# Loading a quarter of the Toeplitz rows in the first 20 ring blocks, and copying the other quarters on chip

## The chip, the cores and the metric

The kernel runs on one core of a Trainium2 chip. The metric is the device time of one execution in microseconds (us). Besides the unprofiled runs there is one profiled execution, from whose trace all rows below are read. The engines are PE (TensorE), ACT (ScalarE), DVE (VectorE), POOL (GpSimd) and SP (SyncE, which here only issues DMAs).

## The reference

Two layers with a residual each, on x of shape (128 batch, 128 time, 512 channels):

```
# layer 0: causal convolution of length 128 per channel (weights cond[k, d]), projection, state recurrence
conv = conv_b + sum(x_pad[:, k:k+L, :] * cond[k] for k in range(128))
proj = conv @ Wp + bp                    # 512 -> 2*64
B_t, C_t = softplus(proj[..., :64]), tanh(proj[..., 64:])
u = x @ Ws + bs
state = decay * state + dt * B_t * u_t;  y_t = C_t * state      # over time
x = x + (y @ Wo + bo)
# layer 1: tanh recurrence over time, h0 = cond
h = tanh(h @ Wh + x_t @ Wx + b)
x = x + h
```

The change touches only the convolution. For one channel d it is a matrix product over time: out[b, l] = sum over p of x_rev[p, b] * T[p, l], where T[p, l] is element p + l of a row of 256 numbers (127 zeros, the 128 weights of the channel reversed, one zero). T is 128 x 128; entries with p + l < 127 are zero, and a row further down is the row above it moved one column to the left.

## The kernel before

The first part of the kernel convolves, transposes and projects. Channels are taken in four chunks c of 128. A chunk is loaded in 16 ring blocks of CH = 8 channels, so there are 64 blocks n = 0 to 63. The ring in SBUF has RING = 4 slots; block n lies in slot n % 4. Each slot holds two halves: `t_part`, the Toeplitz matrices of the eight channels (128 partitions x 1024 floats, 512 KB), and `x_part`, the reversed inputs of the eight channels (512 KB). The Toeplitz rows are read from a small array `hankel` in HBM by a DMA whose rows overlap (`toeplitz`), so that 512 KB are written for very few distinct bytes. Channels are interleaved in pairs (index i), so a row of a pair is 256 floats, and a block has 4 pairs (index j).

SP issues both loads of a block with `load_ring`: first the Toeplitz rows (L254), then x (L255). The first four blocks are issued at once, with a small load `vec` after block 1 and Wp (`wp_f`, L261) after block 3. Block n from 4 on is issued when PE has finished block n - 4 (`conv_done`). Later in the same queue come the weights of the other layers, after blocks 20, 24 and 28. Before, both loads of a slot count on one semaphore, `ring_loaded`.

PE multiplies in `convolution(c, m)`: four channels d into one PSUM bank `CONV[m % 4]`, each channel one f32 matmul of x (weights) with T (moving), which the trace shows as two instructions at L672. A block is two such banks, 16 instructions. m runs over BANKS = 32 for a chunk. Before bank m PE waits until bank m - 4 was emptied. In chunk 0 nothing else runs on PE: `for m in range(BANKS): convolution(0, m)`. ACT empties the even banks (`copy_conv`, L383) and DVE the odd ones (L501), in order, into `conv`.

After chunk 0 PE waits for Wp and its split into a high and a low half (`wp_ready`, made by POOL at L311 and L313), and then, for c = 0 to 2 and each m, runs `turn(c, m)` (four transposes of the finished chunk, L687), `convolution(c + 1, m)` and `project(c, m - 1)` (three matmuls of 512 columns, L700 to L703). ACT and DVE copy and split the turned banks and add the projections. The order on each engine is written out by hand, with semaphore waits. Chunk 3 is turned and projected last, and a loop over 32 groups of 4 time steps (the recurrences) makes up the rest of the time from about 260 us on.

At the start DVE and ACT also compute a few rates from `vec` (L487 to L496, L376, L378), and POOL makes the identity matrix (L305, L307). The function `kernel` lays the inputs out on the host, among them `x_rev`.

Of the kernel before, what the change touches and what calls it, by code (L numbers as in the profile page):

```python
# [8 lines left out]
ALU = mybir.AluOpType  # L9
ACT = mybir.ActivationFunctionType  # L10

BATCH = 128
TIME = 128
D = 512
N = 64
P = 128
KC = D // P
RING = 4
CH = 8
PER_BANK = 4  # L20
BANKS = P // PER_BANK
# [4 lines left out]
LAST = KC - 1  # L26
# [2 lines left out]
SLOTS = 4  # L29
PAIRS = BANKS // 2  # L30
LAG = 2
LOAD = 2 * 16
DMA = 16


def wait(engine, sem, value):

    if not isinstance(value, int) or value > 0:
        engine.wait_ge(sem, value)


def build(nc, x_rev, x_dtb, hankel, h0_t, vectors, Wp, Ws, Wo, Wx, Wh, b, out):
# [6 lines left out]
    with ctx:  # L49
# [3 lines left out]
        def sem(name):  # L53
            return ctx.enter_context(nc.semaphore(name))
# [90 lines left out]
        def f(ap):  # L145
            return ap.bitcast(F32)

        def t_part(slot):
            return ring[:, slot, 0].rearrange("p (j l i) -> p j l i", j=CH // 2, i=2)

        def x_part(slot):
            return ring[:, slot, 1].rearrange("p (d b) -> p d b", d=CH)

# [22 lines left out]
        def turned_slot(c, m):  # L176
            return turned[:, (BANKS * c + m) % SLOTS]

        ring_loaded = [sem(f"ring_loaded{i}") for i in range(RING)]
        conv_done = sem("conv_done")  # L180
        conv_copied_act = sem("conv_copied_act")
        conv_copied_dve = sem("conv_copied_dve")
# [59 lines left out]
        def toeplitz(n):  # L242

            return bass.AP(hankel.tensor, n * (CH // 2 * 4 * P), [[2, P], [4 * P, CH // 2], [1, 2 * TIME]])

        block = ctx.enter_context(nc.Block())

        @block.sync
        def _(sp):
            def load_ring(n, slot):
                sp.dma_start(ring[:, slot, 0].rearrange("p (j k) -> p j k", j=CH // 2), toeplitz(n)).then_inc(ring_loaded[slot], DMA)  # L254
                sp.dma_start(x_part(slot), x_rev[:, bass.ds(n * CH, CH), :]).then_inc(ring_loaded[slot], DMA)  # L255

            for n in range(RING):
                load_ring(n, n)
                if n == 1:
                    sp.dma_start(vec[:], vectors).then_inc(vec_loaded, DMA)  # L260
            sp.dma_start(wp_f[:], Wp.rearrange("(c p) n -> p c n", p=P)).then_inc(wp_loaded, DMA)  # L261
            for n in range(RING, D // CH):
                sp.wait_ge(conv_done, CH // PER_BANK * (n - RING + 1))
                load_ring(n, n % RING)
                if n == 20:
                    sp.dma_start(wo_f[0:N, :], Wo).then_inc(ws_wo_loaded, DMA)
                    sp.dma_start(ws_f[:], Ws.rearrange("(c p) n -> p c n", p=P)).then_inc(ws_wo_loaded, DMA)
                if n == 24:
                    sp.dma_start(wx_f[:], Wx.rearrange("(c p) n -> p c n", p=P)).then_inc(wx_loaded, DMA)
                if n == 28:  # L270
                    sp.dma_start(wh_f[:], Wh.rearrange("(c p) n -> p c n", p=P)).then_inc(wh_loaded, DMA)
                    sp.dma_start(h0_f[:], h0_t.rearrange("(c p) b -> p c b", p=P)).then_inc(h0_loaded, DMA)

            def load_x(g, slot):
                sp.dma_start(x_f[slot][:], x_dtb[:, bass.ds(g * G, G), :].rearrange("(c p) t b -> p c t b", p=P))\
                  .then_inc(x_loaded[slot], DMA)


            sp.wait_ge(conv_done, BANKS * KC - 4)
            load_x(0, 0)  # L280


            sp.wait_ge(turn_done, BANKS * LAST + 24)
            load_x(1, 1)
            sp.dma_start(b_rows[:], b.partition_broadcast(P)).then_inc(b_loaded, DMA)

            def stores_and_loads(g, par, first, last, q):
                if not (last or (isinstance(g, int) and g == GROUPS - 2)):

                    sp.wait_ge(x1_ready, KC * (g + 1))  # L290
                    load_x(g + 2, par)

                for s in range(0, G, 1 if last else G):
                    n = 1 if last else G
                    sp.wait_ge(out_ready, G * g + s + n)
                    sp.dma_start(out[:, bass.ds(g * G + s, n), :].rearrange("(c p) t b -> p c t b", p=P),
                                 x1_f[par][:, :, s:s + n]).then_inc(stored[par], DMA)

            groups(sp, stores_and_loads)
            sp.wait_ge(stored[0], DMA * (GROUPS // 2))  # L300
            sp.wait_ge(stored[1], DMA * (GROUPS // 2 - 1 + G))

        @block.gpsimd
        def _(pool):
# [2 lines left out]
            nc.gpsimd.affine_select(out=ident[:], in_=ident[:], compare_op=ALU.not_equal, fill=1.0, base=0,  # L307
                                    pattern=[[-1, P]], channel_multiplier=1).then_inc(ident_ready, 1)

            pool.wait_ge(wp_loaded, DMA)  # L310
            nc.gpsimd.tensor_copy(wp_hi[:], wp_f[:, 0:LAST]).then_inc(wp_ready, 1)  # L311
            pool.wait_ge(wp_ready, 1)
            nc.gpsimd.tensor_tensor(wp_lo[:], wp_f[:, 0:LAST], f(wp_hi[:]), ALU.subtract).then_inc(wp_ready, 1)  # L313

            pool.wait_ge(ws_wo_loaded, 2 * DMA)
            nc.gpsimd.tensor_copy(ws_hl[:, :, 0:N], ws_f[:]).then_inc(pool_step, 1)
            pool.wait_ge(pool_step, 1)
# [54 lines left out]
        def _(act):  # L372

            nc.scalar.preload_act_table_set("natural_log_exp_and_others")
            act.wait_ge(rate_step, 1)
            nc.scalar.activation(rates_e[:], rates[:, 0:2], ACT.Exp).then_inc(rate_act, 1)  # L376
            act.wait_ge(rate_act, 1)
# [2 lines left out]
            def copy_conv(c, m):  # L380

                act.wait_ge(conv_done, BANKS * c + m + 1)
                nc.scalar.copy(conv_room(c, m), conv_out(c, m))\  # L383
                  .then_inc(conv_copied_act, 1)

            def copy_turned(c, m):

                act.wait_ge(turn_done, BANKS * c + m + 1)
                out = turned_slot(c, m) if c == LAST else turned_hl[:, 0, m % 2]
                nc.scalar.activation(out, turn_bank(c, m)[:], ACT.Identity, bias=conv_b[:, c:c + 1])\  # L390
                  .then_inc(turn_copied, 1)

            act.wait_ge(vec_loaded, DMA)
            for m in range(0, BANKS, 2):
                copy_conv(0, m)
            for c in range(KC - 1):
                for m in range(BANKS):
                    copy_turned(c, m)
                    copy_conv(c + 1, m)
            nc.scalar.preload_act_table_set("exp_and_others")  # L400

# [81 lines left out]

        @block.vector
        def _(dve):
            dve.wait_ge(vec_loaded, DMA)
            nc.vector.scalar_tensor_tensor(out=rates[:, 0:2], in0=logs, scalar=-1.0, in1=logs, op0=ALU.mult, op1=ALU.min)\  # L487
              .then_inc(rate_step, 1)
# [10 lines left out]
            def copy_conv(c, m):  # L499
                dve.wait_ge(conv_done, BANKS * c + m + 1)  # L500
                nc.vector.tensor_copy(conv_room(c, m), conv_out(c, m))\  # L501
                  .then_inc(conv_copied_dve, 1)
# [15 lines left out]
                  .then_inc(turn_rest, 1)  # L518

            for m in range(1, BANKS, 2):  # L520
                copy_conv(0, m)
            for c in range(KC - 1):
                for m in range(BANKS):
                    turn_rest_of(c, m)
                    if m > 0:
                        add_proj(c, m - 1)
                add_proj(c, BANKS - 1)
                if c == 1:

                    dve.wait_ge(ws_wo_loaded, 2 * DMA)  # L530
                    nc.vector.tensor_scalar(wo_f[N:P, :], wo_f[0:N, :], rates_e[0:N, 1:2], None, ALU.mult)\
                      .then_inc(wo_scaled, 1)
                    dve.wait_ge(wo_scaled, 1)
                    nc.vector.tensor_scalar(wo_f[0:N, :], wo_f[0:N, :], rates_e[0:N, 1:2], None, ALU.mult)\
                      .then_inc(wo_scaled, 1)
# [118 lines left out]
        def _(pe):  # L654
            pe.wait_ge(ident_ready, 1)

            def convolution(c, m):

                for d in range(PER_BANK * m, PER_BANK * (m + 1)):
                    n = P // CH * c + d // CH  # L660
                    slot = n % RING
                    if d % CH == 0:
                        pe.wait_ge(ring_loaded[slot], LOAD * (n // RING + 1))
                    if d % PER_BANK == 0 and m >= 4:

                        if c > 0:
                            pe.wait_ge(conv_copied_act, BANKS // 2 + BANKS * (c - 1) + m - 3)
                        elif m % 2 == 0:
                            pe.wait_ge(conv_copied_act, (m - 4) // 2 + 1)
                        else:  # L670
                            pe.wait_ge(conv_copied_dve, (m - 4) // 2 + 1)
                    mm = nc.tensor.matmul(CONV[m % 4][:, bass.ts(d % PER_BANK, TIME)], x_part(slot)[:, d % CH],  # L672
                                          t_part(slot)[:, d % CH // 2, :, d % 2], start=True, stop=True)
                mm.then_inc(conv_done, 1)
# [189 lines left out]
```

## Time and profile before

| what | value |
|---|---|
| median of 3 runs | 1185.26 us (1185.19 to 1185.41) |
| the profiled execution | 1186.63 us, its span 1184.5 us |
| busy PE, DVE, ACT, POOL | 1158.7, 681.2, 562.3, 332.7 us |
| Toeplitz loads | 64 of 512 KB |
| x loads of the ring | 64 of 512 KB |

The span runs from the first to the last instruction of the trace; the time of the execution is longer by what lies around it. Busy time of PE is modelled and its matmuls overlap, so idle time and the distance between starts say more than the length of one matmul. Idle time of an engine that nobody waits for costs nothing.

### The profile page before, as it was taken

The page shows a single profiled execution, that of the slowest core. Times are in us where ns is not written, and L with a number is a line of the kernel's source. Part 1 is how long each engine was busy: PE and PEld are TensorE (multiplying, and loading weights), DVE is VectorE, ACT ScalarE, POOL GpSimd, SP SyncE. Part 2 cuts the span into 40 slices and gives each one's busy share as a digit, 9 for nine tenths or more (in the row PEclk, how much of TensorE's full clock was granted, in tenths as well). Part 3 has the DMA queues.
Part 4 walks back from the last instruction along what each step waited for, and adds up shares of the span by engine and source line. Part 5 has one row for each costly group of instructions (what it writes and reads, how often), then busy time and mean ns, then how long its engine had stood idle before and what let it go on. Part 6 is the DMA issues. An engine that isn't in the chain of part 4 may idle for free.

```text
span 1184.5 us, 15976 instructions
## 1 busy us (share of the span) xinstructions
PE 1158.7 (98%) x5984; PEld 968.5 (82%) x5984; DVE 681.2 (58%) x1078; ACT 562.3 (47%) x816; POOL 332.7 (28%) x180
## 2 busy tenths in 40 slices
PE   6799999999999999999999999999999999999997
PEld 5799999985788888888888888888888888888886
DVE  1367677667555555555655656555555555555553
ACT  2255666575354544535354445454454545453431
POOL 0000005021233444433333333344433333333340
PEclk9999999999999999999999999999999999999999
DMA  9988877730122222222222222222223222222202
GB/s 350 385 290 285 254 259 247 243 99 20 61 72 72 72 71 71 92 91 91 80 71 71 71 71 71 71 71 71 87 91 91 86 71 71 71 71 71 72 36 71
DMA packets 81424, 137.97 MB, mean 116 GB/s; under 512 B 3888, under 2 KB 39728, under 8 KB 81392
## 3 DMA queue, kind: packets, MB, share of 16 engines
q1 hardware_dynamic: 81392, 137.51, 35.4%
q8 instruction: 24, 0.39, 0.1%
q14 instruction: 8, 0.07, 0.0%
HBM read 103.95 MB, written 33.55 MB: 116 GB/s over the span
## 4 chain that ended last, share of the span: by engine, by line
PE 95%; DMA 3%; DVE 1%; POOL 0%; issue 0%; ACT 0%; SPq 0%; POOLq 0%; DVEq 0%
PE bank L753 10%; PE bank L761 10%; PE bank L762 10%; PE bank L747 10%; PE bank L765 10%; PE bank L746 10%; PE bank L672 9%; PE bank L687 5%; PE bank L801 5%; DMA ring<-x_rev 3%; PE bank L722 3%; PE bank L728 3%; PE bank L736 2%; PE bank L737 2%; PE bank L701 2%; PE bank L703 2%
## 5 line engine op out<-in xcount | busy, mean ns | idle before, releaser
L354 POOL TENSOR_TENSOR x_lo<-x_f,x_hi 128x512 fp32r<-128x512 f32 x128 | 161.7, 1290 | 588.2 <-ACT x_hi L433 588.1
L460 ACT ACTIVATE h_f<-z_f 128x512 f32<-128x512 f32 x128 | 80.9, 632 | 296.7 <-DVE z_f L624 296.7
L761 PE MATMUL bank<-wh_hi,hT_hi 128*128 128x512 f32 x512 | 200.8, 392 | 0.0
L762 PE MATMUL bank<-wh_lo,hT_hi 128*128 128x512 f32 x512 | 199.9, 390 | 0.0
L747 PE MATMUL bank<-wx_lo,x_hi 128*128 128x512 f32 x512 | 199.7, 390 | 0.0
L746 PE MATMUL bank<-wx_hi,x_hi 128*128 128x512 f32 x512 | 199.6, 390 | 0.0
L633 DVE TENSOR_TENSOR hT_lo<-bank,hT_hi 128x512 fp32r<-128x512 f32 x128 | 88.6, 692 | 186.8 <-ACT hT_hi L464 186.8
L624 DVE TENSOR_TENSOR z_f<-bank,b_rows 128x512 f32<-128x512 f32 x128 | 88.6, 692 | 132.2 <-PE bank L765 129.2
L672 PE MATMUL bank<-ring 128*128 128x128 f32 x1024 | 138.6, 280 | 16.9 <-DMA ring<-x_rev 16.9
L348 POOL TENSOR_TENSOR x_lo<-x_f,x_hi 128x2048 fp32r<-128x2048 f32 x32 | 147.6, 4612 | 1.5 <-PE bank L672 1.4
L672 PEld LDWEIGHTS bank<-ring 128*128 128x128 f32 x1024 | 129.5, 194 | 19.3 <-DMA ring<-x_rev 12.7
L753 PE MATMUL bank<-wx_hi,x_lo 128*128 128x512 f32 x512 | 144.7, 404 | 0.4 <-POOL x_lo L354 0.4
L765 PE MATMUL bank<-wh_hi,hT_lo 128*128 128x512 f32 x512 | 137.0, 389 | 0.0
L464 ACT CAST hT_hi<-bank 128x512 fp32r<-128x512 f32 x128 | 75.1, 587 | 94.5 <-PE bank L801 94.5
L761 PEld LDWEIGHTS bank<-wh_hi,hT_hi 128*128 128x128 f32 x512 | 96.1, 188 | 26.2 <-ACT hT_hi L464 6.1
L433 ACT CAST x_hi<-x_f 128x512 fp32r<-128x512 f32 x128 | 79.6, 622 | 74.3 <-DVE x_f L591 71.8
L765 PEld LDWEIGHTS bank<-wh_hi,hT_lo 128*128 128x128 f32 x512 | 96.1, 188 | 20.4
L746 PEld LDWEIGHTS bank<-wx_hi,x_hi 128*128 128x128 f32 x512 | 96.1, 188 | 20.2 <-issue 0.2
L747 PEld LDWEIGHTS bank<-wx_lo,x_hi 128*128 128x128 f32 x512 | 96.1, 188 | 20.2 <-issue 0.2
L762 PEld LDWEIGHTS bank<-wh_lo,hT_hi 128*128 128x128 f32 x512 | 96.2, 188 | 19.7 <-issue 0.2
L753 PEld LDWEIGHTS bank<-wx_hi,x_lo 128*128 128x128 f32 x512 | 91.2, 188 | 17.2 <-POOL x_lo L354 0.6
L516 DVE SCALAR_TENSOR_TENSOR turned_hl<-bank,vec,turned_hl 128x512 fp32r<-128x512 f32 x96 | 72.1, 751 | 50.9 <-ACT turned_hl L390 50.9
(77 smaller groups left out, 1595.0 us busy)
## 6 DMA issues: line engine op xcount, KB each, us to landing
ring<-hankel SPq DMA_DIRECT2D x64, 512.0 KB, 4.5
ring<-x_rev SPq DMA_DIRECT2D x64, 512.0 KB, 5.5
x_f<-x_dtb SPq DMA_DIRECT2D x32, 1024.0 KB, 8.2
out<-x_f SPq DMA_DIRECT2D x31, 1024.0 KB, 5.4
wx_f<-Wx SPq DMA_DIRECT2D x1, 1024.0 KB, 8.0
wh_f<-Wh SPq DMA_DIRECT2D x1, 1024.0 KB, 7.9
out<-x_f SPq DMA_DIRECT2D x4, 256.0 KB, 2.2
wp_f<-Wp SPq DMA_DIRECT2D x1, 384.0 KB, 9.8
```

The source lines that it names most:

```text
L348: nc.gpsimd.tensor_tensor(x_lo[:], x_f[par][:], f(x_hi[:]), ALU.subtract).then_inc(xlo_ready, 1)
L354: nc.gpsimd.tensor_tensor(x1_lo[:, c], x1_f[par][:, c], f(x1_hi[:, c]), ALU.subtract)\
L460: nc.scalar.activation(h_f[:], z_f[:], ACT.Tanh).then_inc(h_ready, 1)
L624: nc.vector.tensor_tensor(z_f[:], ZB[s % 2][:], b_rows[:], ALU.add).then_inc(zsum_ready, 1)
L633: nc.vector.tensor_tensor(hT_lo[:], turned_h, f(hT_hi[:]), ALU.subtract).then_inc(htlo_ready, 1)
L672: mm = nc.tensor.matmul(CONV[m % 4][:, bass.ts(d % PER_BANK, TIME)], x_part(slot)[:, d % CH], t_part(slot)[:, d % CH // 2, :, d % 2], star ...
L746: nc.tensor.matmul(z, x1_hi[:, k, s], wx_hi[:, k], start=(k == 0), stop=False)
L747: nc.tensor.matmul(z, x1_hi[:, k, s], wx_lo[:, k], start=False, stop=False)
L753: mm = nc.tensor.matmul(z, x1_lo[:, k, s], wx_hi[:, k], start=False, stop=stop and k == KC - 1)
L761: nc.tensor.matmul(z, hT_hi[:, k], wh_hi[:, k], start=False, stop=False)
L762: nc.tensor.matmul(z, hT_hi[:, k], wh_lo[:, k], start=False, stop=False)
L765: mm = nc.tensor.matmul(z, hT_lo[:, k], wh_hi[:, k], start=False, stop=stop and k == KC - 1)
```

## The change

For blocks n < SHIFTED = 20 SP loads only the lowest quarter of the Toeplitz rows (32 rows, 128 KB). The other three quarters are the same numbers moved by 32, 64 and 96 columns, with zeros in front: POOL copies 96 of the 128 columns to the next quarter, DVE 64 to the one after and ACT 32 to the last. Their zero parts are written once per slot by DVE (`zero`), since the copies never touch them. In odd blocks the order of the quarters over the partitions is reversed, so the loaded quarter lies on partitions 96 to 127 in even blocks and on 0 to 31 in odd ones; the host reverses the quarters of `x_rev` in these blocks to match. The semaphore of a slot becomes two, one for the rows and one for x, and PE also waits for the three copies. Two banks ahead in the work of ACT and DVE stand the copies of block n + 2. POOL does its copies in order from the start, with the split of Wp put after blocks 10 and 13.

```diff
+SHIFTED = 20
+Q = P // 4
...
+        def toeplitz_low(n):
+            return bass.AP(hankel.tensor, n * (CH // 2 * 4 * P) + 2 * (P - Q), [[2, Q], [4 * P, CH // 2], [1, 2 * TIME]])
+        def quarter(n, q):
+            at = 3 - q if n % 2 else q
+            return slice(Q * at, Q * (at + 1))
+        def shift_to(n, q):
+            return t_part(n % RING)[quarter(n, q), :, (3 - q) * Q:P]
+        def shift_from(n, q):
+            return t_part(n % RING)[quarter(n, 3), :, 0:(q + 1) * Q]
...
             def load_ring(n, slot):
-                sp.dma_start(ring[:, slot, 0].rearrange("p (j k) -> p j k", j=CH // 2), toeplitz(n)).then_inc(ring_loaded[slot], DMA)
-                sp.dma_start(x_part(slot), x_rev[:, bass.ds(n * CH, CH), :]).then_inc(ring_loaded[slot], DMA)
+                t_rows = ring[:, slot, 0].rearrange("p (j k) -> p j k", j=CH // 2)
+                if n < SHIFTED:
+                    sp.dma_start(t_rows[quarter(n, 3)], toeplitz_low(n)).then_inc(t_loaded[slot], DMA)
+                else:
+                    sp.dma_start(t_rows, toeplitz(n)).then_inc(t_loaded[slot], DMA)
+                sp.dma_start(x_part(slot), x_rev[:, bass.ds(n * CH, CH), :]).then_inc(x_part_loaded[slot], DMA)
...
# POOL
-            pool.wait_ge(wp_loaded, DMA)
-            nc.gpsimd.tensor_copy(wp_hi[:], wp_f[:, 0:LAST]).then_inc(wp_ready, 1)
-            pool.wait_ge(wp_ready, 1)
-            nc.gpsimd.tensor_tensor(wp_lo[:], wp_f[:, 0:LAST], f(wp_hi[:]), ALU.subtract).then_inc(wp_ready, 1)
+            def shift(n):
+                slot = n % RING
+                if n < RING:
+                    pool.wait_ge(t_zeroed, n + 1)
+                pool.wait_ge(ident_ready, 1)
+                wait(pool, shifted_pool, n)
+                if n > 10:
+                    pool.wait_ge(wp_ready, 2 if n > 13 else 1)
+                pool.wait_ge(t_loaded[slot], DMA * (n // RING + 1))
+                nc.gpsimd.tensor_copy(shift_to(n, 2), shift_from(n, 2)).then_inc(shifted_pool, 1)
+            for n in range(SHIFTED):
+                shift(n)
+                if n == 10:
+                    pool.wait_ge(wp_loaded, DMA)
+                    pool.wait_ge(shifted_pool, n + 1)
+                    nc.gpsimd.tensor_copy(wp_hi[:], wp_f[:, 0:LAST]).then_inc(wp_ready, 1)
+                if n == 13:
+                    pool.wait_ge(wp_ready, 1)
+                    pool.wait_ge(shifted_pool, n + 1)
+                    nc.gpsimd.tensor_tensor(wp_lo[:], wp_f[:, 0:LAST], f(wp_hi[:]), ALU.subtract).then_inc(wp_ready, 1)
+            pool.wait_ge(shifted_pool, SHIFTED)
...
# ACT
+                nc.scalar.copy(shift_to(n, 0), shift_from(n, 0)).then_inc(shifted_act, 1)
+            shift(0)
+            shift(1)
...
             for m in range(0, BANKS, 2):
+                shift(m // 2 + 2)
                 copy_conv(0, m)
             for c in range(KC - 1):
                 for m in range(BANKS):
                     copy_turned(c, m)
+                    if c == 0 and m % 2 == 0 and m // 2 + BANKS // 2 + 2 < SHIFTED:
+                        shift(m // 2 + BANKS // 2 + 2)
                     copy_conv(c + 1, m)
...
# DVE
+            def zero(slot):
+                nc.vector.memset(t_part(slot)[quarter(slot, 0), :, 0:3 * Q], 0.0)
+                nc.vector.memset(t_part(slot)[quarter(slot, 1), :, 0:2 * Q], 0.0)
+                nc.vector.memset(t_part(slot)[quarter(slot, 2), :, 0:Q], 0.0).then_inc(t_zeroed, 1)
...
+                nc.vector.tensor_copy(shift_to(n, 1), shift_from(n, 1)).then_inc(shifted_dve, 1)
+            zero(0)
+            zero(1)
+            shift(0)
+            zero(2)
+            shift(1)
+            zero(3)
...
             for m in range(1, BANKS, 2):
+                shift(m // 2 + 2)
                 copy_conv(0, m)
             for c in range(KC - 1):
                 for m in range(BANKS):
                     turn_rest_of(c, m)
+                    if c == 0 and m % 2 == 0 and m // 2 + BANKS // 2 + 2 < SHIFTED:
+                        shift(m // 2 + BANKS // 2 + 2)
...
# PE
-                        pe.wait_ge(ring_loaded[slot], LOAD * (n // RING + 1))
+                        pe.wait_ge(t_loaded[slot], DMA * (n // RING + 1))
+                        if n < SHIFTED:
+                            pe.wait_ge(shifted_pool, n + 1)
+                            pe.wait_ge(shifted_dve, n + 1)
+                            pe.wait_ge(shifted_act, n + 1)
+                        pe.wait_ge(x_part_loaded[slot], DMA * (n // RING + 1))
...
# kernel(), on the host
+    x_rev = x.transpose(1, 2, 0)[::-1].copy()
+    for n in range(1, SHIFTED, 2):
+        block = x_rev[:, n * CH:(n + 1) * CH]
+        block[:] = block.reshape(4, Q, CH, BATCH)[::-1].reshape(P, CH, BATCH)
```

## Rows read from the trace of the kernel before

**Rows 1.** The chain that ended last, 0 to 60 us: start, length, what.

```profile
by line: DMA ring<-x_rev 54.7%; PE bank L672 32.9%; PE bank L687 4.2%; SPq L254 2.6%; issue 1.2%; DVE conv L501 1.2%; PE bank L703 0.8%; PE bank L701 0.8%; PE bank L700 0.8%
...
1.26 5.19 DMA ring<-x_rev
...
6.59 10.34 PE bank L672 x64
...
50.14 2.09 PE bank L672 x16
```

**Rows 2.** Busy time by stretch: length, engines (x instructions), PEclk, DMA share, GB/s.

```profile
0.00:6.59 6.59, 0.00 (x0) 0.03 (x1) 0.00 (x0) 1.28 (x1) 0.70 (x6) 1.00 0.69 205
6.59:16.95 10.36, 10.33 (x64) 10.02 (x64) 2.62 (x7) 2.64 (x6) 0.86 (x2) 1.00 1.07 388
16.95:52.25 35.30, 24.98 (x192) 22.63 (x192) 8.30 (x12) 7.04 (x12) 1.20 (x1) 1.00 1.06 395
52.25:257.00 204.75, 203.90 (x1438) 191.62 (x1439) 140.53 (x193) 122.32 (x193) 20.45 (x12) 1.00 0.77 255
```

**Rows 3.** Timeline of the queue of SP, Toeplitz loads and one x load.

```profile
10.38 0.38 SPq L254 DMA_DIRECT2D ring<-hankel  x1
...
13.14 0.37 SPq L254 DMA_DIRECT2D ring<-hankel  x1
...
16.95 0.37 SPq L254 DMA_DIRECT2D ring<-hankel  x1
...
25.84 0.37 SPq L254 DMA_DIRECT2D ring<-hankel  x1
...
29.55 0.37 SPq L254 DMA_DIRECT2D ring<-hankel  x1
...
52.25 0.37 SPq L254 DMA_DIRECT2D ring<-hankel  x1
52.66 0.51 SPq L255 DMA_DIRECT2D ring<-x_rev  x1
```

**Rows 4.** PE at L672: one block, then matmul durations (min/median/max) at 6.5:12 and 12:17.

```profile
18.50 2.08 PE L672 MATMUL bank<-ring 128*128 128x128 f32 x16 [1.58 <-DMA ring<-x_rev]
...
L672 PE MATMUL bank<-ring x25: 415/415/554, 6.6 to 11.8; 128*128 128x128 f32 x25
...
L672 PE MATMUL bank<-ring x41: 273/275/415, 11.6 to 16.6; 128*128 128x128 f32 x41
```

**Rows 5.** DMA issues, median us to landing: x at 20:50, both loads at 100:150.

```profile
ring<-x_rev SPq DMA_DIRECT2D x11, 512.0 KB, 8.9
...
ring<-hankel SPq DMA_DIRECT2D x12, 512.0 KB, 4.0
ring<-x_rev SPq DMA_DIRECT2D x12, 512.0 KB, 4.9
```

**Rows 6.** Groups by form, POOL, DVE and ACT operations nearest to the added ones.

```profile
L311 POOL CAST wp_hi<-wp_f 128x576 fp32r<-128x576 f32 x1 | 0.7, 664 | 14.5 <-DMA wp_f<-Wp 14.5
L313 POOL TENSOR_TENSOR wp_lo<-wp_f,wp_hi 128x576 fp32r<-128x576 f32 x1 | 1.4, 1400 | 0.1
L534 DVE TENSOR_SCALAR wo_f<-wo_f,rates_e 64x512 f32<-64x512 f32 x1 | 0.5, 485 | 0.0
L433 ACT CAST x_hi<-x_f 128x512 fp32r<-128x512 f32 x4 | 2.5, 619 | 0.7 <-DVE x_f L591 0.5
L501 DVE COPY conv<-bank 128x512 f32<-128x512 f32 x15 | 10.4, 691 | 27.7 <-PE bank L672 27.7
L383 ACT COPY conv<-bank 128x512 f32<-128x512 f32 x16 | 9.4, 585 | 32.3 <-PE bank L672 32.3
L487 DVE SCALAR_TENSOR_TENSOR rates<-vec 128x2 f32<-128x2 f32 x1 | 0.2, 161 | 9.7 <-DMA vec<-vectors 9.7
```

**Rows 7.** Stretches of the fill: length, PE busy, PEclk, DMA share, GB/s.

```profile
2.00:4.00 2.00, 0.00 (x0) 1.00 0.91 238
4.00:6.46 2.46, 0.00 (x0) 1.00 1.01 329
```

More of the change, by code:

```diff
@@ L31 @@
 LAG = 2
-LOAD = 2 * 16
 DMA = 16
@@ L177, in turned_slot @@
             return turned[:, (BANKS * c + m) % SLOTS]
-        ring_loaded = [sem(f"ring_loaded{i}") for i in range(RING)]
+        t_loaded = [sem(f"t_loaded{i}") for i in range(RING)]
+        x_part_loaded = [sem(f"x_part_loaded{i}") for i in range(RING)]
+        t_zeroed = sem("t_zeroed")
+        shifted_pool = sem("shifted_pool")
+        shifted_dve = sem("shifted_dve")
+        shifted_act = sem("shifted_act")
         conv_done = sem("conv_done")
@@ L374, in _, with shift @@
             nc.scalar.preload_act_table_set("natural_log_exp_and_others")
+            def shift(n):
+                slot = n % RING
+                if n < RING:
+                    act.wait_ge(t_zeroed, n + 1)
+                act.wait_ge(t_loaded[slot], DMA * (n // RING + 1))
+                nc.scalar.copy(shift_to(n, 0), shift_from(n, 0)).then_inc(shifted_act, 1)
+            shift(0)
+            shift(1)
             act.wait_ge(rate_step, 1)
@@ L485, in _, with shift @@
         def _(dve):
+            def zero(slot):
+                nc.vector.memset(t_part(slot)[quarter(slot, 0), :, 0:3 * Q], 0.0)
+                nc.vector.memset(t_part(slot)[quarter(slot, 1), :, 0:2 * Q], 0.0)
+                nc.vector.memset(t_part(slot)[quarter(slot, 2), :, 0:Q], 0.0).then_inc(t_zeroed, 1)
+            def shift(n):
+                slot = n % RING
+                if n < RING:
+                    dve.wait_ge(t_zeroed, n + 1)
+                dve.wait_ge(t_loaded[slot], DMA * (n // RING + 1))
+                nc.vector.tensor_copy(shift_to(n, 1), shift_from(n, 1)).then_inc(shifted_dve, 1)
[5 more added lines that the diff above has]
+            zero(3)
             dve.wait_ge(vec_loaded, DMA)
@@ L834, in halves @@
         return np.concatenate([a, a], axis=0)
+    x_rev = x.transpose(1, 2, 0)[::-1].copy()
+    for n in range(1, SHIFTED, 2):
+        block = x_rev[:, n * CH:(n + 1) * CH]
+        block[:] = block.reshape(4, Q, CH, BATCH)[::-1].reshape(P, CH, BATCH)
     arrays = {
-        "x_rev": x.transpose(1, 2, 0)[::-1],
+        "x_rev": x_rev,
         "x_dtb": x.transpose(2, 1, 0),
```

## The prediction, made before the changed kernel ran

> **What bounds the kernel now.** I start with the chain that ended last, from the start of the span [rows 1]. Over the first 60 us more than half of it is a DMA, the load of x into the ring; after that it is PE, line after line. So there are two regimes, and the windows cut at their border say so in numbers [rows 2]: from 16.95 to 52.25 us PE is busy 24.98 of 35.30 us while the DMA share is 1.06 at 395 GB/s; from 52.25 to 257 us PE is busy 203.90 of 204.75 us with the DMA share at 0.77. The first sixteen ring blocks (the convolution of channels 0 to 127) are thus bound by the transfers, everything later by PE. The change touches the first twenty blocks only, so its worth must come out of the first 52 us.
>
> How much is there to be had? The queue of SP [rows 3] issues the Toeplitz load of block n+4 as soon as PE has finished block n, so its starts are a clock of PE's blocks. Block 0 takes 6.59 to 10.38 us, block 1 to 13.14, blocks 2 and 3 together 3.81 us (13.14 to 16.95), 1.91 each, and there PE has no idle time. The last one, block 15, ends at 52.25. Its 16 matmuls take 2.08 us from the first start to the modelled end, each group preceded by an idle piece that a DMA ended [rows 4]. The longer blocks 0 and 1 are not waits: their matmuls have a median of 415 ns against 275 ns later [rows 4], although the granted clock reads 1.00 in every stretch [rows 2]. I keep that cost as it is: the first four blocks take 10.34 us [rows 1] in both kernels, as PE starts from rest in both.
>
> **The change, part by part.**
>
> *Bytes.* A block is 512 KB of Toeplitz rows and 512 KB of x, 1.05 MB; at 395 GB/s that is 2.65 us, against 1.91 us of PE. Twelve blocks are 31.8 us and the 0.39 MB of Wp 1.0 us; the other 2.5 us of the 35.3 are pauses. With a quarter of the rows, 128 KB, a block is 0.655 MB, 1.66 us at the same rate. This is less than 1.91, so PE becomes the limit, if no latency does.
>
> *The latency of the ring.* A slot is refilled when PE finishes block n and is needed three PE blocks later, after 5.73 us. Where the queue was not full (100 to 150 us) the Toeplitz load lands 4.0 us after its issue and x 4.9 us after its own, which comes 0.41 us later [rows 3, 5]; while it was full x took 8.9 us [rows 5]. The 0.393 MB saved stand in front of x, worth 1.0 us. I take x landing 0.41 + 4.9 - 1.0 = 4.3 us after the first issue, some 1.4 us to spare, and the rows at 4.0 - 1.0 = 3.0 us.
>
> *The three copies.* They lie between the landing of the rows and PE. POOL has the largest, 768 elements on 32 partitions. No row shows a copy that changes partitions. Its cast of 576 elements took 664 ns, which gives 0.89 us for 768; its subtraction of 576 took 1400 ns, which gives 1.87 us [rows 6]. I take 0.9, since cast and copy are the same one-input operation, and keep 1.9 as the far end. DVE copies 512 elements: 0.49 us by its SBUF to SBUF operation of that length. ACT copies 256: at most the 0.62 us of its 512-element cast [rows 6]. So the block is ready 3.0 + 0.9 + 0.1 = 4.0 us after issue by the copies, before x at 4.3: hidden by the x load. If that cover went, 1.7 us of slack to PE's need remain. As work per block of 1.91 us the engines have room: DVE has one bank copy of 0.69 us and ACT one of 0.59 [rows 6], POOL nothing but the split of Wp (0.66 and 1.40 us, now put behind blocks 10 and 13). The second delays POOL's copy of block 14 by about 0.5 us, inside the slack. PE asks for the split only after block 15.
>
> *What is queued behind the copies.* ACT and DVE wait for the rows of block n+2 before they empty the banks of block n. Those rows land 3.1 us after the end of block n-2, the bank is full after 2.9 to 3.8 us, the copies add at most 0.6, and PE wants the bank back at block n+2, 5.7 us on. The delay, at most 0.9 us for ACT, reaches nobody. At the border to the next stage blocks 18 and 19 are copied between the first turns, where ACT and DVE are busy 122 and 141 of 205 us [rows 2]; I cost it at nothing, at most some 0.6 us if a copy stands before the first bank of that stage.
>
> *Zeroing.* DVE needs 161 ns for two elements and 691 ns for 512 [rows 6], so 1.04 ns per element and 0.16 fixed. The memsets of 768, 512 and 256 elements cost 2.08 us per slot at that price; they could take half of it (DVE's SBUF to SBUF operation of 512 took 0.49), which would not matter, as x is then the last. DVE starts at about 0.75, so slots 0 and 1 are clear at 4.9, its copy of block 0 ends at 5.4; slot 2 at 7.5, copy of block 1 at 8.0, slot 3 at 10.1. Block 1 is wanted at 5.5 + 3.8 = 9.3 and block 2 at 12.1, so only block 0 can feel it.
>
> *The start.* x of block 0 landed at 6.45 and PE began at 6.59 [rows 1]. Between 4.00 and 6.46 us the DMA ran at 329 GB/s, and 2.00 to 4.00 at 238 [rows 7]. 0.393 MB fewer in front are 1.2 us at the former: x lands at 5.25. With DVE's copy at 5.4 PE begins at about 5.5, 1.1 us earlier.
>
> *More waits.* PE waits five times instead of once before a block. In the stage after 52.25 us PE passes several waits for each bank and is idle 0.85 us in 204.75 [rows 2]; I take nothing; 0.85 us spread over 48 blocks would be 0.3 us for these sixteen, the upper bound.
>
> *The sum.* 5.5 + 10.34 + 12 x 1.91 = 38.8 us for the end of block 15, against 52.23 now: 13.4 us. Against that I set 0.9 us for what stays uncovered of two things. One is that the transfers pause now and then: the interval 25.84 to 29.55 is 3.7 us where its neighbours have 2.6 [rows 3], and with PE as the limit the ring absorbs a pause of 1.1 us only if the slack is full. The other is the price of a 32-partition transfer (below). Gain 12.5 us. After that nothing is tied to absolute time; the later stages are bound by PE and move up rigidly. The profiled execution of before took 1186.63 us, span 1184.5; the sum gives a span of 1172.0. It lies 1.37 us above the median of the runs, 1185.26, which goes to 1172.8.
>
> **The rivals.**
>
> *The DMA stays the limit.* If 128 KB on 32 partitions run at half the rate, a block is 1.33 + 0.66 = 1.99 us, which exceeds 1.91; that alone costs 12 x 0.08 = 1.0 us, and then the pauses, 2.5 us, are paid in full. Gain 13.4 - 1.0 - 2.5 = 9.9 us, 1175.4. For it: the DMA share was above 1 all through this stage. Against it: successive blocks land on opposite quarters of the partitions, and x follows at once. The Trainium skill has a rule that speaks for this rival (SBUF — State Buffer, "Door 1: The DMA port swizzle"): a transfer onto 32 adjacent partitions reaches 8 of the 16 ports of the memory, and about half the bandwidth. No row here shows such a transfer; by the rule the sum would be the one of this rival, without it 1171.9.
>
> *The rows are no cheaper.* If the time of this load goes by its fixed part or by few engines and not by its bytes, a block still takes 2.6 us and nothing changes: 1184 to 1186. Against it: in the full queue both loads together took 2.65 us per block, which is what their bytes give.
>
> *POOL becomes the limit, partly.* Its chain is 3.5 us until the first rows, sixteen copies P with 0.06 between, the Wp split (2.1) and the last block (1.9): 8.5 + 16 P. It passes 38.8 from P = 1.9 us on. At P = 2.3 the end is 45.3 and the gain 6.9 us, 1178.4; at 2.7 it is gone.
>
> *Slower.* The same mechanism at a higher price: if a POOL copy onto other partitions costs over 2.75 us (3.6 ns per element, three times its cast), block 15 ends later than now; at 3.5 us it ends at 64.5, 12 us later, 1197.5. For it: no row has this form. Against it: nothing but the nearest rows, 1.15 and 2.4 ns per element.
>
> **How the numbers follow.** PE-bound as summed 0.64, DMA still the limit 0.20, POOL partly 0.07, no change (rows no cheaper, or POOL near 2.7) 0.04, slower 0.05. Within 0.2%, 2.4 us, a measurement can't tell this kernel from no change, so faster 0.91, same 0.04, slower 0.05. The time is that of the first case, 1172.8. Its lower end: no allowance (0.9), a start 0.3 earlier and a cheaper hand-over to the next stage (0.8): 1170.8. The upper end takes in the DMA rival and 2.1 us beyond it, should the transfers on few partitions cost more than double (2.16 instead of 1.99 us per block): 1177.5.
>
> **What would show it.** Between 16 and 40 us PE should be busy above 95% with the DMA share near 0.85 to 1.0 and about 340 GB/s; SP's issues 1.9 to 2.0 us apart; the first matmul at 5.5; the first turn at 40 instead of 53.1. POOL's copy should show about 0.9 us, DVE's 0.5, ACT's under 0.6, the memsets 0.96, 0.69 and 0.43. The prediction is wrong if the wait before PE's blocks is ended by the x load with the DMA share still above 1 (ports), or by POOL with copies back to back, or if PE waits for an emptied bank behind a copy.

## The result

The changed kernel takes 1178.1 us (median of 6 runs, 1176.82 to 1180.91) against 1185.28 us before; the ratio is 0.9939 with a 95% interval of 0.9926 to 0.9952, so it is faster, by 7.2 us instead of the 12.5 forecast, and 0.6 us outside the range. Its profiled execution took 1177.63 us, its span 1175.8, which is 8.7 us less than the span before. The profiled execution of before lay 1.4 us above its median and this one 0.5 us below, so the two traces differ by more than the medians do.

### The profile page after: what moved, and what is told of

The parts are those of the page before. It is cut to its first block, busy times and chain, and to the rows that moved or that the text cites. A ratio compares the mean times of both kernels' runs of the same rounds, so it can differ in the third digit from the quotient of the medians.

```text
span 1175.8 us, 16134 instructions
## 1 busy us (share of the span) xinstructions
PE 1157.7 (98%) x5984; PEld 969.3 (82%) x5984; DVE 697.0 (59%) x1110; ACT 569.6 (48%) x836; POOL 350.8 (30%) x200
## 4 chain that ended last, share of the span: by engine, by line
PE 96%; DVE 2%; DMA 1%; POOL 0%; issue 0%; ACT 0%; POOLq 0%; SPq 0%; DVEq 0%
PE bank L836 10%; PE bank L844 10%; PE bank L845 10%; PE bank L830 10%; PE bank L848 10%; PE bank L829 10%; PE bank L755 10%; PE bank L770 5%; PE bank L884 5%; PE bank L805 3%; PE bank L811 3%; PE bank L819 2%; PE bank L820 2%; PE bank L784 2%; PE bank L786 2%; PE bank L783 2%
```

## The profile after

Busy time by stretch, changed kernel, cut at the first matmul, the end of block 3 and the end of block 15 (columns as in [rows 2]):

```profile
0.00:5.37 5.37, 0.00 (x1) 0.03 (x1) 3.48 (x8) 1.69 (x2) 1.52 (x7) 1.00 0.67 192
5.37:15.71 10.34, 9.83 (x66) 9.66 (x67) 8.68 (x18) 3.87 (x10) 3.48 (x5) 1.00 1.05 323
15.71:41.29 25.58, 23.36 (x192) 22.16 (x191) 13.47 (x24) 10.89 (x24) 13.42 (x14) 1.00 1.00 301
41.29:246.00 204.71, 202.66 (x1421) 190.56 (x1422) 139.83 (x194) 122.22 (x194) 21.68 (x14) 0.99 0.77 252
```

Blocks 4 to 15 take 25.58 us instead of 35.3. PE is busy 23.36 of them, 91% where it was 71% before, but the DMA share is still 1.00, at 301 GB/s where before 395 GB/s moved [rows 2]: the transfers are as busy as ever and carry less. The last stretch was given the length of the one in [rows 2], so its 204.71 us say nothing of the speed; it holds fewer matmuls (1421 against 1438), and the border below shows why. The new operations cost about what was expected, the memsets less; groups by form, 0 to 62 us:

```profile
L346 POOL COPY ring<-ring 32x768 f32<-32x768 f32 x20 | 18.3, 913 | 26.0 <-DMA ring<-hankel 25.6 <-POOL wp_hi L353 0.2 <-POOL wp_lo L357 0.2
L553 DVE COPY ring<-ring 32x512 f32<-32x512 f32 x20 | 9.4, 470 | 12.9 <-DMA ring<-hankel 12.7
L425 ACT COPY ring<-ring 32x256 f32<-32x256 f32 x20 | 8.1, 403 | 21.7 <-DMA ring<-hankel 21.6
L544 DVE MEMSET ring<- 32x768 f32 x4 | 2.8, 698 | 1.6 <-PEq L942 1.0 <-issue 0.6
L545 DVE MEMSET ring<- 32x512 f32 x4 | 1.9, 485 | 0.6
L546 DVE MEMSET ring<- 32x256 f32 x4 | 1.1, 272 | 0.4
```

All three copies wait for the Toeplitz load, not for each other. The timeline of PE at the border to the second stage:

```profile
43.34 0.93 PE L770 MATMUL bank<-ident,conv 128*128 128x128 f32 x4 [2.07 <-DVE conv L576]
44.05 1.91 PE L755 MATMUL bank<-ring 128*128 128x128 f32 x8
45.77 1.06 PE L770 MATMUL bank<-ident,conv 128*128 128x128 f32 x4
46.61 1.42 PE L755 MATMUL bank<-ring 128*128 128x128 f32 x8
47.78 0.48 PE L783 MATMUL bank<-turned_hl,wp_hi 128*128 128x512 f32 x1
```

The first transposes wait 2.07 us for DVE's last bank copy. Before the change the same wait was 0.88 us:

```profile
53.10 0.83 PE L687 MATMUL bank<-ident,conv 128*128 128x128 f32 x4 [0.88 <-DVE conv L501]
```

What DVE and the queue of SP did meanwhile in the changed kernel (DVE copies the rows of block 17, L553, and only then the bank, L576):

```profile
36.23 0.33 SPq L278 DMA_DIRECT2D ring<-hankel  x1
...
42.05 0.42 DVE L553 COPY ring<-ring 32x512 f32<-32x512 f32 x1 [1.36 <-DMA ring<-hankel]
...
42.50 0.69 DVE L576 COPY conv<-bank 128x512 f32<-128x512 f32 x1
```

The rows landed 5.8 us after their issue, not 3.0. And the eight convolution matmuls after the first transposes take 1.91 us instead of 1.08. The clock says why (length, PE busy, PEclk, DMA share, GB/s):

```profile
43.00:44.00 1.00, 0.67 (x4) 0.96 0.97 241
44.00:45.00 1.00, 1.00 (x7) 0.50 1.06 313
45.00:46.00 1.00, 1.00 (x7) 0.50 0.98 214
46.00:47.00 1.00, 1.00 (x6) 0.50 0.56 205
47.00:48.00 1.00, 1.00 (x9) 0.84 0.09 33
```

For over 3 us the granted clock was 0.50, the lower of its two levels (1.2 GHz), after PE had stood idle for 2.07 us.

What the border cost is the time from the end of block 15 to the end of the span: 1175.8 - 41.29 = 1134.5 us, where it was 1184.5 - 52.25 = 1132.25 us before. That is 2.3 us more, and the rest of the kernel did not move up rigidly.

## The experiments

The measure used below is the time from the end of block 3 to the end of block 15, read in the queue of SP as the distance between the x issues of blocks 7 and 19, which follow these ends; twelve blocks. In the changed kernel:

```profile
16.08 0.44 SPq L281 DMA_DIRECT2D ring<-x_rev  x1
...
41.66 0.43 SPq L281 DMA_DIRECT2D ring<-x_rev  x1
```

**The same bytes onto all partitions.** For blocks 4 to 19:

```diff
+        def one_pair(n):
+            return bass.AP(hankel.tensor, n * (CH // 2 * 4 * P), [[2, P], [4 * P, 1], [1, 2 * TIME]])
...
-                if n < SHIFTED:
+                if RING <= n < SHIFTED:
+                    sp.dma_start(t_rows[:, 0:1], one_pair(n)).then_inc(t_loaded[slot], DMA)
+                elif n < SHIFTED:
                     sp.dma_start(t_rows[quarter(n, 3)], toeplitz_low(n)).then_inc(t_loaded[slot], DMA)
```

> For blocks 4 to 19 this kernel loads the same 128 KB in the same 128 pieces of 1 KB, but onto all 128 partitions (one channel pair of four) instead of 32; three pairs keep old rows, so that part of the convolution is left out of the computation. Copies, waits and x loads are as in the changed kernel, where block 4 to block 15 took 25.6 us (2.13 per block) at 320 GB/s with the DMA share above 1. Theory (a 32-partition transfer runs at half rate, 0.72 us instead of 0.33): a block needs 1.66 us of DMA, PE is the limit at 1.93, block 15 ends at 38.6 to 39.3 us instead of 41.3, the DMA share falls below 0.95, and the time is 2 to 4 us under the changed kernel. Rival (the load costs by its pieces or a fixed part, wherever it lands): no change, block 15 ends at 41.3 and the DMA share stays above 1.

Measured: 1178.13 us, 29.45 us for the twelve blocks, block 15 ending at 44.5. Not faster, so the partitions alone are not the cause. The trace is blurred by a spell of clock 0.50 from about 22.5 to 26 us, after a wait of 1.83 us; but from 16 to 41 us its DMA share was 0.98 at 274 GB/s, so the transfers hardly stood still in it and were not faster either (301 GB/s in the changed kernel).

**Bank copies before the rows of block 17.** On ACT and on DVE:

```diff
             for m in range(1, BANKS, 2):
-                shift(m // 2 + 2)
+                if m < BANKS - 1:
+                    shift(m // 2 + 2)
                 copy_conv(0, m)
+            shift(17)
```

> The changed kernel with one order turned round: ACT and DVE empty the last two banks of the first chunk before they copy the rows of block 17. In the changed kernel the first transposes waited 2.07 us, for DVE's bank copy behind its row copy, whose rows landed at 42.02; after that wait the granted clock of PE was 0.50 from about 44 to 47.3 us. Theory (the wait at the border comes from this order, and the low clock follows the wait): the wait falls to 0.9 us as before the change, worth 1.2 us, the clock stays at 1.00 and its stretch gives back another 1.5 us; time 2.5 us under the changed kernel. Rival (the rows of block 17 and 18 are needed at once anyway, so the wait moves to the next bank, and the clock falls on its own): within 0.5 us of the changed kernel.

Measured: 1175.85 us (1175.33 to 1176.64), ratio to before 0.9924 (0.9907 to 0.9940), 2.25 us under the changed kernel. PE at the border:

```profile
42.43 0.82 PE L774 MATMUL bank<-ident,conv 128*128 128x128 f32 x4 [0.87 <-DVE conv L578]
43.09 1.08 PE L759 MATMUL bank<-ring 128*128 128x128 f32 x8
```

The wait is 0.87 us as before the change, the matmuls are at full speed, and the clock is 1.00 from 40 to 52 us. After block 15 this kernel takes 1173.8 - 41.58 = 1132.2 us, the time of the kernel before, so the 2.3 us of the border are gone, and the trace confirms the theory. Its twelve blocks took 26.47 us.

**No alternation**, `at = q` in `quarter`, x as before:

> The changed kernel without the alternation: the loaded quarter lies on partitions 96 to 127 in every block. Theory (the half of the partitions that is not written lies idle during such a transfer, whichever it is, since the x load of all partitions comes between two of them): no change, 320 GB/s and block 15 ending at 41.3 within 0.5 us. Rival (neighbouring transfers overlap, so that alternation gives back part of the loss): 0.72 us become up to 1.0 per load, block 15 ends 2 to 4 us later.

Measured: 1178.88 us, 28.91 us for the twelve blocks against 25.58, block 15 ending at 44.2. In its trace the rival is right in direction: alternation gives 0.28 us per block against the changed kernel's trace, 0.20 against the trace with the bank copies first. The rates from 16 to 41 us, 288 against 304 GB/s, would make it 0.12, so the size is known only as 0.1 to 0.3. In the time 0.8 us shows, less than the spread of either kernel's runs. Part of the loss is hidden at the border: there the clock stayed at 1.00 after a wait of 1.9 us, where the changed kernel's fell, and the time after block 15 is 1133.2 us instead of 1134.5.

**Half of the rows onto partitions 32 to 95:**

```diff
-            at = 3 - q if n % 2 else q
+            at = (0, 3, 1, 2)[q]
...
-                    sp.dma_start(t_rows[quarter(n, 3)], toeplitz_low(n)).then_inc(t_loaded[slot], DMA)
+                    sp.dma_start(t_rows[Q:3 * Q], toeplitz_low(n)).then_inc(t_loaded[slot], DMA)
```

(Here `toeplitz_low` reads 64 rows, POOL's copies are left out, and the host puts the rows of `x_rev` in the same order.)

> Half of the Toeplitz rows is loaded (256 KB in 256 pieces of 1 KB) onto partitions 32 to 95, and DVE and ACT copy the other two quarters; POOL copies nothing. Same output. Theory (half rate for 32 partitions of one end; 32 to 95 take part in both halves and run at the full rate): 256 KB cost 0.66 us, a block 1.99 us of DMA, as much as with a quarter (2.05), though at 390 GB/s; block 15 ends at 40 to 41.3, and the rows are ready 0.5 us earlier without POOL's 0.91 us copy; 0 to 1.5 us under the changed kernel. Rival (cost by pieces or bytes whatever the partitions): the load costs twice 0.72, a block 2.77 us, and the time is that of the kernel before or more, 1185 to 1188.

Measured: 1178.86 us, 27.58 us for the twelve blocks (2.30 each), 349 to 371 GB/s. Twice the bytes cost 0.17 us more per block, far from the 2.77 us of the rival. But 2.30 is not the theory's 1.99 either, block 15 ends at 43.4 instead of 40 to 41.3, and the wait at the border was 2.8 us, so the time is not under the changed kernel's.

**Prices, one extra load at a time.** These seven kernels have the bank copies first, and each was executed once. Each issues one more load behind the x load of blocks 4 to 15, into `bc`, which is not yet in use; DVE waits for all of them after its last copies of the first chunk:

```diff
                 sp.dma_start(x_part(slot), x_rev[:, bass.ds(n * CH, CH), :]).then_inc(x_part_loaded[slot], DMA)
+                if RING <= n < 16:
+                    sp.dma_start(<a part of bc[:, bass.ts(n, CH * P)]>, <source>).then_inc(extra_loaded, DMA)
```

> The kernel with the bank copies first, and behind the x load of each of blocks 4 to 15 the same x load once more, into a buffer that nothing reads. 12 extra loads of 512 KB; in the base kernel block 15 ended at 41.6 us with the transfers the limit. Theory A (bytes at the full rate cost 395 GB/s, the 32-partition load is the dear one): 1.33 us each, block 15 ends at 57.6. Theory C (new: x is read in 128 rows of 4 KB that lie 256 KB apart in HBM, and this load is the slow one, near 1.95 us, while the Toeplitz rows cost little beside it): 23 us more, block 15 ends near 65, the extra bytes moving at about 270 GB/s.

> The same with the whole Toeplitz load (512 KB, 128 partitions, 512 pieces of 1 KB) of the block as the extra one, for blocks 4 to 15. Theory A: 1.33 us each, block 15 ends at 57.6 as with an extra x. Theory C: 0.7 us each, since the kernel before moved 384 KB more per block in only 0.5 us more; block 15 ends near 50.

> The same with the quarter load (128 KB onto 32 partitions) as the extra one, for blocks 4 to 15. Theory A (half rate or a fixed part): 0.66 to 0.75 us each, block 15 ends near 50. Theory C: 0.17 to 0.35 us each, block 15 ends at 43.7 to 45.8.

> The kernel with the bank copies first, with 128 KB more of the Toeplitz array for blocks 4 to 15, onto all 128 partitions (one piece of 1 KB each, all from one 2 KB stretch of HBM), into a buffer that nothing reads. The steady block was 2.82 us with an extra quarter load onto 32 partitions and 3.50 with an extra x; solved, a quarter load costs 0.71 us, an x load 1.39. What is open is why the quarter costs twice its bytes (0.33). Where it lands (32 partitions): this one costs 0.33 to 0.4, a block 2.5 us. Where it comes from (many reads of a few KB of HBM): 0.71 or more, a block 2.8 us or more. A fixed cost of each DMA: 0.71, 2.8 us.

> As the last, but the extra 128 KB are 128 pieces of 1 KB from the x array, each from another place in HBM, onto the 32 partitions of the quarter. Where it lands: 0.71 us, a block 2.8. Where it comes from: 0.33 to 0.4, a block 2.5. A fixed cost of each DMA: 0.71, 2.8.

> As the last, but the 128 pieces of 1 KB from the x array go onto 128 partitions, one each. Where it lands, and where it comes from: both say 0.33 to 0.4, a block 2.5 us. A fixed cost of each DMA: 0.71, 2.8 us.

> As the last, but only 16 KB extra (16 pieces of 1 KB, one for each DMA engine, onto 16 partitions). Its bytes are 0.04 us. Where it lands, and where it comes from: 0.04 to 0.1 us, a block 2.2 us as in the base kernel. A fixed cost of each DMA: 0.3 to 0.5, a block 2.5 to 2.7 us.

The marks of the three that decide, quarter load (first pair), 128 KB of x onto 32 partitions (second), 128 KB of x onto 128 partitions (third), each from its own trace:

```profile
15.57 0.43 SPq L282 DMA_DIRECT2D ring<-x_rev  x1
...
49.90 0.43 SPq L282 DMA_DIRECT2D ring<-x_rev  x1
```

```profile
15.82 0.43 SPq L282 DMA_DIRECT2D ring<-x_rev  x1
...
50.06 0.43 SPq L282 DMA_DIRECT2D ring<-x_rev  x1
```

```profile
16.01 0.43 SPq L282 DMA_DIRECT2D ring<-x_rev  x1
...
46.27 0.43 SPq L282 DMA_DIRECT2D ring<-x_rev  x1
```

The base is the mean of the changed kernel (25.58), the bank-first kernel (26.47) and the one with the tiny load (26.42), 26.2 us; these show what one profile is worth, about half a us in twelve blocks or 0.05 per load. Price = (time - 26.2) / 12:

| extra load | twelve blocks, us | price, us | price by rate, us |
|---|---|---|---|
| x, 512 KB, 128 partitions, pieces of 4 KB | 41.39 | 1.27 | 1.27 |
| all Toeplitz rows, 512 KB, 128 partitions | 45.10 | 1.58 | 1.61 |
| quarter of the rows, 128 KB, 32 partitions | 34.33 | 0.68 | 0.66 |
| one pair of the rows, 128 KB, 128 partitions | 33.29 | 0.59 | 0.58 |
| 128 KB of x in 1 KB pieces, 32 partitions | 34.24 | 0.67 | 0.62 |
| 128 KB of x in 1 KB pieces, 128 partitions | 30.26 | 0.34 | 0.33 |
| 16 KB of x, 16 partitions | 26.42 | 0.02 | 0.03 |

The last column is a check that does not hang on where the twelve blocks begin and end: the bytes of a block with its extra load over the rate from 16 to 41 us, less the 2.16 us of the bank-first kernel (0.655 MB at 304 GB/s). It matters for two reasons. Two of the traces have a spell of clock 0.50 (128 KB of x onto 32 partitions from 29 to about 32.5 us, all Toeplitz rows from 44 to about 50.5 us). And only eleven of the twelve extra loads are issued ahead of an x load that PE waits for. The rates of the bank-first kernel and of the four loads of 128 KB, in the order of the table (packets, bytes, rate, and how many packets are under each size):

```profile
DMA packets 3278, 7.61 MB, mean 304 GB/s; under 512 B 358, under 2 KB 1784, under 8 KB 3275
DMA packets 3846, 6.97 MB, mean 279 GB/s; under 512 B 429, under 2 KB 2721, under 8 KB 3845
DMA packets 3909, 7.16 MB, mean 287 GB/s; under 512 B 434, under 2 KB 2740, under 8 KB 3908
DMA packets 3870, 7.08 MB, mean 283 GB/s; under 512 B 429, under 2 KB 2717, under 8 KB 3869
DMA packets 4387, 7.92 MB, mean 317 GB/s; under 512 B 486, under 2 KB 3113, under 8 KB 4386
```

There is no fixed price of a DMA (0.02), and the x load costs its bytes (1.33 expected), so theory C is dead. The full Toeplitz load, 1.58, missed both of its expectations (1.33 and 0.7). 128 KB cost 0.34 us only when they go onto all partitions and come from the x array. Onto 32 partitions they cost twice that from either source; from the overlapping rows they cost 1.7 times that even onto all partitions; both at once still cost only 0.68. So the first experiment failed because it lifted one limit and ran into the other.

What it is in the overlapping rows that costs is not shown: their pieces lie within a few KB, overlap, and start 8 bytes apart, while the pieces of x start at multiples of 1 KB. No run changes one of these without the others.

**x in one piece of HBM per block**, `x_rev[n]` from an array of 64 blocks:

> The kernel with the bank copies first, and x laid out by the host so that each block's 512 KB lie in one piece of HBM (64 blocks of 128 rows of 4 KB); same output. Theory A: nothing changes, DMA share above 1 and about 310 GB/s, block 15 ends at 41.6, 1175.9 us. Theory C: the x load costs 1.3 us, PE becomes the limit, block 15 ends at 38.5 to 39.3 us, the DMA share falls under 0.95, and the time is 1173 to 1174; the later stage stays bound by PE.

Measured: 1177.37 us (1175.87 to 1179.5), 30.08 us for the twelve blocks at 277 GB/s. Slower in its trace than rows 256 KB apart, but that execution was the slowest of four, 2.1 us above their median, and the ranges of the times overlap. It is not faster, so theory C is refuted again.

**A cheap load in the place of the quarter**, the 0.34 us form, for blocks 4 to 19:

> The kernel with the bank copies first; for blocks 4 to 19 the Toeplitz load is replaced by 128 KB from the x array, one piece of 1 KB onto each of 128 partitions, the form that cost 0.31 us as an extra load. All copies and waits stay; the convolution of these blocks is computed from wrong rows. From the end of block 3 to the end of block 15 it took 26.5 us in the base kernel (2.2 per block). Theory (nothing but the double price of the quarter load kept PE from being the limit): DMA 1.55 us per block, PE at 1.93, 23.2 us for the twelve, block 15 ends at 38.9, 2.5 to 3.3 us under the base kernel's 1175.9. Rival (latency, the row copies behind their loads, or pauses hold the ring back as well): still 2.1 or more per block, within 1.5 us of the base kernel.

Measured: 1174.56 us (1173.78 to 1174.84), 24.34 us for the twelve blocks (2.03 each). Stretches of 16 to 41 us of this kernel and, second, of the bank-first kernel:

```profile
16.00:41.00 25.00, 23.12 (x195) 22.32 (x194) 14.05 (x25) 11.36 (x25) 13.04 (x14) 1.00 0.92 315
```

```profile
16.00:41.00 25.00, 22.96 (x186) 21.64 (x186) 13.70 (x24) 11.29 (x25) 13.68 (x14) 1.00 1.03 304
```

The DMA share falls to 0.92, and PE runs six blocks in a row at 1.9 us each:

```profile
12.47 11.50 PE L764 MATMUL bank<-ring 128*128 128x128 f32 x96 [0.70 <-POOL ring L351]
24.58 11.35 PE L764 MATMUL bank<-ring 128*128 128x128 f32 x96 [0.61 <-DMA ring<-x_rev]
36.74 3.94 PE L764 MATMUL bank<-ring 128*128 128x128 f32 x32 [0.81 <-DMA ring<-x_rev]
```

The first row starts at block 2, so its pause, ended by POOL's copy, lies before the twelve blocks. In these PE is the limit, as the sum had it, but for two pauses of 0.61 and 0.81 us that an x load ended: 12 x 1.91 + 1.42 = 24.34. The kernel is 1.3 us under the bank-first kernel. That time is within what the rival said, the 2.03 us per block lie between the theory's 1.93 and the rival's 2.1. All the row copies run in this kernel too, so they are not what slowed the transfers.

**The kernel before, with rows written out in HBM** (no overlapping reads):

> The kernel before the change, but the Toeplitz rows of blocks 0 to 19 come from an array in which the host wrote every row out, so 512 pieces of 1 KB are read from 512 different places instead of overlapping ones; same output. An extra full load of overlapping rows had cost 1.55 us, an extra x load of the same bytes 1.24. Theory (overlapping reads are dear in the full load too): 0.3 us less per block, 35.3 us from block 3 to block 15 become 31.6, 4 to 5 us under 1185.3. Rival (only the small loads suffer, from reading few places at once): within 1 us of 1185.3.

Measured: 1184.4 us against 1184.82, ratio 0.9997 (0.9987 to 1.0006): no difference, as the rival said. In the full load beside x the overlapping reads are not a limit of the kernel.

The twelve blocks took 33.14 us in this trace, not the 35.3 of [rows 2]:

```profile
17.03 0.94 SPq L255 DMA_DIRECT2D ring<-x_rev  x1
...
50.17 0.51 SPq L255 DMA_DIRECT2D ring<-x_rev  x1
```

This is a difference of two executions rather than of two kernels. The profiled one of before was 2.5 us longer as a whole (1186.63 against 1184.1), all of it ahead of the end of block 15 (52.25 against 49.76), and after that both took 1132.2 us. So the trace that the prediction was worked out from probably shows a first stage about as much too long as its execution lay above the median, 1.4 us.

**Half of the rows, written out, bank copies first:**

> Half of the rows onto partitions 32 to 95, from written-out rows, with two copies and the bank copies first; same output. By the prices found, 256 KB onto both halves of the partitions from separate places cost 0.62 us, as much as the quarter onto 32 (0.65). Theory (two separate prices, which do not add): 1.9 to 2.2 us per block, time within 1.5 us of the kernel with the bank copies first, 1175.9. Rival (the load still costs by its source or its partitions beyond that): 2.3 per block as with overlapping rows, 1177 to 1178.

Measured: 1175.38 us (1174.9 to 1175.85), 25.72 us for the twelve blocks (2.14 each), 371 GB/s. Within 0.5 us of the quarter with the same order, as the two prices say, and 0.16 us less per block than the half from overlapping rows.

## Why the prediction was wrong

*Right:* the transfers bounded the first sixteen blocks of the kernel before and nothing else, and the change paid only there. The start was at 5.37 us (5.5 predicted), the end of block 3 at 15.71 (15.84). POOL's copy took 0.91 us (0.89), DVE's 0.47, ACT's 0.40; the memsets took 1.46 us per slot, less than the 2.08 priced. No wait of PE on the copies in the changed kernel's steady blocks, so neither POOL rival nor "no cheaper" came true.

*The step that failed first* is the price of the quarter load, taken at the rate of the full queue (0.33 us, a block of 1.66). It costs 0.68, twice that, so a block is 1.27 + 0.68 = 1.95 us of DMA: above PE's 1.91, as in the first rival, which had 1.99. The slack that was to absorb a late x load is gone with it. The twelve blocks took 25.58 us, 2.7 more than 12 x 1.91; I had set 0.9 against it, so 1.8 us are missing here. The rule of the Trainium skill that stood beside this rival (SBUF — State Buffer, "Door 1: The DMA port swizzle") agrees with the pair 0.67 against 0.34 us, same source, 32 against 128 partitions. It does not cover the 0.59 us of overlapping rows onto 128 partitions. What the price was worth is seen in the cheap load: 1.3 us in the time, 2.1 us in the traces of the twelve blocks (24.34 against 26.47).

*The second step*, and the larger one, is the border, costed at nothing to 0.6 us. I had the landing of rows at 3.0 us after issue, from a queue that is not full; in one that stays full it was 5.8. So DVE's copy of the rows of block 17 stood before the last bank copy: 2.07 us of wait instead of 0.87, and the clock at 0.50 behind it. The claim that the later stages move up rigidly failed with it: they took 2.3 us more (1134.5 against 1132.25), and the other order gives back 2.25 us in the time. A PE wait behind a copy was named among the signs of failure and not priced as a case; without it the result, 1175.85, would have been inside the range. How much of it is the clock is read from one trace each: 1.2 us are the wait, the rest is the slow stretch. That the wait makes the clock fall is likely, not shown, since longer waits in other traces did not.

*The third step* is the base of the sum. It found the end of block 15 as a time of its own (39.7 us), took the gain of 12.5 us from a trace with 52.23, and subtracted that gain from the median, 1.37 us below that execution. But those 1.37 us most likely lay in the very stage that the sum replaced (the trace with written-out rows shows 49.76 for the same point), so a median execution had only some 11.1 us to gain. 1174.56 us, with the price and the border mended, is still 1.8 us above the 1172.8 forecast; this explains about 1.4 of it, as far as two single executions can show. Late loads count too: in the cheap-load trace the first four blocks took 11.00 us instead of 10.34, and the twelve 24.34 instead of the 23.8 allowed.

Two readings behind the 2.5 us of pauses were also wrong. Wp's 1.0 us does not belong in the 35.3 us, since Wp had landed at 16.0 us, before block 3 was done. And the "pauses" were not pauses of the transfers: 395 GB/s over all 35.3 us are 13.9 MB, 1.4 MB more than twelve blocks. The transfers went on, for later blocks too, while PE waited for one x load. Why single x loads come late while the queue moves bytes stays open.

A version that beats both kernels: the change with the bank copies first, 1175.85 us. Half the rows, written out, are as good (1175.38) and need no copy by POOL.

## What to carry to other kernels

Do not price a smaller load by its bytes if its form changes too. Here a quarter of the bytes onto a quarter of the partitions cost twice its share, while half of the bytes onto partitions 32 to 95, from written-out rows, cost no more than the quarter. Measure the price of the new form by adding it once more where the queue is full. A copy that waits for a transfer must not stand in an engine's order ahead of work that the next stage is waiting for, and its landing time is to be taken from the queue at its actual load. If a sum replaces a whole stage by a time of its own, subtract it from the stage of a median execution. Where a stage is bound by one stall, ask also what the clock does after it.

## What the runs showed of the hardware

- Two limits of a 128 KB load that do not add: 32 partitions (0.67 us), overlapping source rows (0.59), both (0.68), neither (0.34); one trace each, two measures.
- 16 KB more per block in a full queue cost 0.02 us: no fixed price of a load there.
- x read as one contiguous 512 KB piece per block was not faster than 128 rows 256 KB apart (30.08 us for twelve blocks at 277 GB/s, against 26.47, one trace each); why is open.
- The granted clock fell to 0.50 after PE had been idle 2.07 us (changed kernel), 1.83 (first experiment), 2.01 (128 KB of x onto 32 partitions), 2.22 (one pair of the rows) and 1.96 (extra x), and stayed there for 3 to 4 us; after 1.99 us (all Toeplitz rows) it stayed for some 6.5 us with further idle time in them. It did not fall after 1.9 us (no alternation), 1.99 (kernel before, ahead of block 15), 2.25 (x in one piece) or 2.8 us (half of the rows, overlapping). Such idle times make it possible, not certain; with the short wait of 0.87 us at the border none was seen there.
